# Reordering the loads, the set-up additions and the late transposes of an embedding-and-cross-layer kernel on one core

## The reference

```python
e = jnp.stack([tbl_0[ids[:, 0]], ..., tbl_25[ids[:, 25]]], axis=1)      # 512 x 26 x 32
x1 = jnp.einsum('bik,bjk,hij->bhk', e, e, W1) + b1[None, :, None]       # 128 features
x2 = jnp.einsum('bik,bjk,hij->bhk', x1, e, W2) + b2[None, :, None]      # 128 features
z = jnp.sum(jnp.concatenate([x1, x2], axis=1), axis=-1)                 # 512 x 256
h = jnp.concatenate([z, dense_ctx], axis=1)                             # 512 x 272
h = jnp.maximum(h @ W_top1 + b_top1, 0.0)                               # 512 x 512
h = jnp.maximum(h @ W_top2 + b_top2, 0.0)                               # 512 x 256
y = h @ W_top3                                                          # 512 x 1
```

## Time and profile before

| | |
|---|---|
| median of 3 runs | 177.65 us (177.57 to 177.9) |
| profiled execution | 177.05 us, of which the span is 175.3 us |
| PE busy | 155.5 us (89% of the span) |
| DVE busy | 117.2 us (67%) |
| ACT busy | 74.5 us (43%) |
| POOL busy | 72.8 us (42%) |
| mean granted TensorE clock | 0.961 of full speed |
| bytes moved | 8.71 MB, nearly all in the first 22 us |

### The profile page before, as it was taken

One profiled execution on the slowest core, in us unless ns is written; L12 is line 12 of the kernel. 1 busy time (PEld: TensorE's weight loads), 2 busy tenths in 40 slices (PEclk: granted clock), 3 DMA queues, 4 the chain that ended last, 5 costly groups with the idle time before them and its releaser, 6 DMA issues.

```text
span 175.3 us, 3331 instructions
## 1 busy us (share of the span) xinstructions
PE 155.5 (89%) x1273; PEld 147.0 (84%) x1273; DVE 117.2 (67%) x371; ACT 74.5 (43%) x188; POOL 72.8 (42%) x80
## 2 busy tenths in 40 slices
PE   6549999920999968999899999989999998999995
PEld 6449999910999967999799999979999997999993
DVE  5073748999979994699866669985666996432000
ACT  0205454800595543065555406455540645753022
POOL 2605065545665584545565455466555300000000
PEclk9978999995599999999999999999999999999999
DMA  3999910000000000001000000000000000000000
GB/s 98 410 399 397 351 46 12 9 8 11 11 11 10 9 11 8 11 9 15 11 8 15 8 9 14 13 11 8 15 8 9 14 0 0 6 0 0 4 0 0
DMA packets 4626, 8.71 MB, mean 50 GB/s; under 512 B 1761, under 2 KB 3425, under 8 KB 4354
## 3 DMA queue, kind: packets, MB, share of 16 engines
q1 hardware_dynamic: 1410, 3.63, 5.6%
q10 hardware_dynamic: 896, 3.68, 5.5%
q0 software_dynamic: 2304, 1.18, 4.8%
HBM read 8.49 MB, written 0.00 MB: 48 GB/s over the span
## 4 chain that ended last, share of the span: by engine, by line
PE 70%; DVE 15%; ACT 6%; DMA 5%; issue 2%; SPq 0%
PE bank L337 14%; DVE folded L680 8%; PE bank L345 8%; PE bank L283 8%; PE bank L350 7%; PE bank L354 7%; PE bank L299 6%; DMA w2t<-in_w2t_dram 5%; PE bank L358 5%; PE bank L377 2%; PE bank L375 2%; ACT diag L504 2%; PE bank L364 2%; PE bank L310 2%; ACT h L512 2%
## 5 line engine op out<-in xcount | busy, mean ns | idle before, releaser
L257 POOL DMA_INDIRECT rows<-in_tbl_dram,idx x72 | 72.0, 1000 | 64.1 <-DMA rows<-in_tbl_dram,idx 45.8
L337 PEld LDWEIGHTS bank<-diag,prod 128*128 128x128 f32 x256 | 30.5, 192 | 2.0 <-issue 1.5
L337 PE MATMUL bank<-diag,prod 128*128 128x108 f32 x256 | 31.4, 276 | 0.5 <-issue 0.2
L669 DVE COPY t<-bank 13x128 f32<-13x128 f32 (+1 forms) x64 | 16.8, 263 | 19.3 <-PE bank L345 18.6
L504 ACT ACTIVATE diag<-prod,quad 128x416 f32<-128x416 f32 (+1 forms) x32 | 17.5, 620 | 17.4 <-DVE prod L632 17.4
L485 ACT COPY t<-bank 128x432 f32<-128x432 f32 x32 | 15.0, 522 | 23.1 <-PE bank L337 23.1
L283 PE MATMUL bank<-small,onehot 128*128 128x256 f32 (+1 forms) x64 | 19.8, 412 | 1.4 <-DVE w1p L617 1.4
L617 DVE TENSOR_TENSOR w1p<-bank,chosen 128x320 f32<-128x320 f32 (+2 forms) x24 | 13.1, 547 | 10.9 <-PE bank L283 10.6
L345 PE MATMUL bank<-diag,prod 128*77 128x64 f32 x256 | 20.1, 230 | 0.0
L345 PEld LDWEIGHTS bank<-diag,prod 128*77 128x77 f32 x256 | 19.4, 149 | 0.0
L492 ACT COPY t<-bank 55x256 f32<-55x256 f32 (+2 forms) x48 | 14.1, 294 | 2.7 <-PE bank L345 2.3
(11 more groups left out here) (71 smaller groups left out, 197.3 us busy)
## 6 DMA issues: line engine op xcount, KB each, us to landing
idb<-in_idt_dram ACTq DMA_DIRECT2D x1, 1536.0 KB, 17.4
rows<-in_tbl_dram,idx POOLq DMA_INDIRECT x72, 2.4
small<-in_small_dram SPq DMA_DIRECT2D x1, 1120.0 KB, 12.1
wt<-in_W_top_dram SPq DMA_DIRECT2D x2, 512.0 KB, 17.5
w2t<-in_w2t_dram ACTq DMA_DIRECT2D x1, 832.0 KB, 8.1
w2t<-in_w2t_dram SPq DMA_DIRECT2D x1, 832.0 KB, 9.5
w1t<-in_w1t_dram ACTq DMA_DIRECT2D x1, 640.0 KB, 13.5
w1p<-in_w1p_dram SPq DMA_DIRECT2D x1, 521.0 KB, 7.4
```

The source lines that it names most:

```text
L257: pool.indirect_dma_start(rows[t][:, f, :], None, tables[f], bass.IndirectOffsetOnAxis(ap=idx[:, t, f:f + 1], axis=0)).then_inc(s_got[t][p ...
L337: mm = nc.tensor.matmul(m0[:, g % GBANK, :, 0:JW], prod[:, G, 0:P], diag[:, G, :, :], start=True, stop=True)
L669: ins = nc.vector.tensor_copy(t1[p0:p0 + HALF, GRAM + slot:GRAM + slot + nb, n], m1[64:64 + HALF, :].rearrange("p (n j) -> p j n", n=NSTEP ...
```

## The change

Loads: the indices come in one transfer; `idb` for tile 0 moves from the head of ACT's queue to behind `w1p` on SP's; `w2t` comes in three pieces, all at the head of ACT's queue. DVE: two memsets of `t1` go to the front, the first `one_hot` behind `w1s` and `chosen`; the additions to `b2x32` and `z1w` go behind tile 0's picks; low and cross_a additions go ahead of `half_a(0)`; the cross_b additions go between `half_b(0)`, `bands(0, 0)` and `bands(0, 1)`; all picks of tile 1 go behind the four `bands` of tile 0. PE: the look-ups of tile 0 stand behind later set-up jobs; the v0 jobs of fields 0 to 12 go behind steps 1 and 2 of tile 0, in banks 6 and 7; the look-ups of tile 1 go behind tile 0's four steps, the last one behind `z1`; `layer3(t - 1)` goes behind `step(t, 0)`, with its `copy_y`. ACT: two spreads ahead of `relu2` and two behind it. POOL: of 18 gathers a tile the waits come after 5, 9, 13 and 18.

```diff
-BURST = 3
+PAUSES = [(0, 8), (0, 12), (1, 20), (2, 25)]
+W2PARTS = [(0, 6), (6, 14), (14, 26)]
-HOME = [RING[q % len(RING)] for q in range(DONE["ctB"])] + [0, 1, 2, 0] + [3, 4, 5, 7] + [0, 1, 2, 0]
+HOME = [RING[q % len(RING)] for q in range(DONE["ctB"])] + [0, 1, 2, 0] + [3, 4, 5, 7] + [6, 7, 6, 7]
-BEHIND = {6: 0, 8: 1, FOLDS - 1: 2, FOLDS: 3, FOLDS + 1: 4, FOLDS + 2: 5}
+BEHIND = {10: 0, 12: 1, FOLDS: 2, FOLDS + 1: 3, FOLDS + 2: 4, FOLDS + 3: 5}
@@ sync
-            sp.dma_start(idx[:, 0, :], io["ids"][:, 0, :]).then_inc(s_idx[0], 16)
+            sp.dma_start(idx[:], io["ids"]).then_inc(s_idx, 16)
             sp.dma_start(w1p[:], io["w1p"]).then_inc(s_w1p, 16)
-            sp.dma_start(w2t[:, 0:HALF, :], io["w2t"][:, 0:HALF, :]).then_inc(s_w2[0], 16)
+            sp.dma_start(idb[:, 0, :], on_all(io["idt"], 0, 1)).then_inc(s_idb[0], 16)
@@ gpsimd
-                        if f > g0 and (f - g0) % BURST == 0:
-                            pool.wait_ge(s_got[t][part], 16 * (f - g0))
+                        if (part, f) in PAUSES:
+                            if part == 2:
+                                pool.wait_ge(s_got[t][1], 16 * (PARTS[1][1] - PARTS[1][3]))
+                            pool.wait_ge(s_got[t][part], 16 * (f + 1 - g0))
-                    pool.wait_ge(s_got[t][part], 16 * (f1 - g0))
@@ tensor, look_up, make and step
+                if t == 1 and pick < 2:
+                    pe.wait_ge(s_sf, len(SETUP))
+                    if x0 == 0:
+                        pe.wait_ge(s_pb, PRODS)
+                    if t and s == 0 and g == GBANK:
+                        pe.wait_ge(s_h2, t * MT2)
@@ tensor, the tiles
                     step(t, s)
-                    if more:
-                        if s == 0 and t == 0:
-                            pe.wait_ge(s_sf, DONE["v1"])
+                    if t and s == 0:
+                        layer3(t - 1)
+                    if t and more:
                         look_up(t + 1, s)
+                    if t == 0 and s in (1, 2):
+                        for q in range(DONE["v1"] + 2 * s - 2, DONE["v1"] + 2 * s):
+                            make(q)
+                pe.wait_ge(s_e0, (t + 1) * STEPS)
                 if t == 0:
-                    pe.wait_ge(s_e0, STEPS - 1)
-                    pe.wait_ge(s_e1, STEPS - 1)
-                    pe.wait_ge(s_eg, STEPS - 1)
-                    for q in range(DONE["v1"], len(SETUP)):
-                        make(q)
-                    pe.wait_ge(s_sf, len(SETUP))
+                    look_up(1, 0)
+                    look_up(1, 1)
                 z2_low(0, 6)
+                if t == 0:
+                    look_up(1, 2)
                 z2_low(6, HALF)
+                if t == 0:
+                    look_up(1, 3)
                 z2_high(t)
+                    look_up(1, 4)
                 z1()
+                if t == 0:
+                    look_up(1, 5)
                 layer1(t)
                 layer2(t)
-                layer3(t)
+            layer3(TILES - 1)
@@ scalar
-            act.dma_start(idb[:, 0, :], on_all(io["idt"], 0, 1)).then_inc(s_idb[0], 16)
-            act.dma_start(w2t[:, HALF:FIELDS, :], io["w2t"][:, HALF:FIELDS, :]).then_inc(s_w2[1], 16)
-            act.dma_start(idx[:, 1:TILES, :], io["ids"][:, 1:TILES, :]).then_inc(s_idx[1], 16)
+            for i, (j0, j1) in enumerate(W2PARTS):
+                act.dma_start(w2t[:, j0:j1, :], io["w2t"][:, j0:j1, :]).then_inc(s_w2[i], 16)
+                    if s == 0 and t:
+                        copy_y(t - 1)
+                    if t == 0 and s in (1, 2):
+                        for q in range(DONE["v1"] + 2 * s - 2, DONE["v1"] + 2 * s):
+                            take(q)
-                    spread(t + 1, 1, range(0, 3))
+                    spread(t + 1, 1, range(0, 2))
                 relu2(t)
-                    spread(t + 1, 1, range(3, QUADS))
+                    spread(t + 1, 1, range(2, QUADS))
@@ vector, tile 0
+            nc.vector.tensor_scalar(b2x32[:], vec[:, 0:1], float(EMB), None, ALU.mult).then_inc(s_pad, 1)
+            nc.vector.tensor_tensor(z1w[:], w1t[:, 0, :, :], w1t[:, 1, :, :], ALU.add).then_inc(s_z1w, 1)
-            half_a(0)
...
+            half_a(0)
             half_b(0)
             cross = cross_b(folded, ct[1])
-            for t in range(TILES):
+            add(cross, 0, False)
+            bands(0, 0)
+            add(cross, 1, True)
+            bands(0, 1)
+            one_hot(1)
+            bands(0, 2)
+            bands(0, 3)
+            for i in range(len(PICKS)):
+                pick(1, i)
+            half_a(1)
+            half_b(1)
+            for t in range(1, TILES):
```

More of the change, by code:

```diff
@@ L180, in arrive @@
         def arrive(t, pick):
-            return bank[6 + pick % 2] if t == 0 else bank[7]
-        s_idx = [sem(f"s_idx{i}") for i in range(2)]
+            return bank[6 + pick % 2] if t < 2 else bank[7]
+        s_idx = sem("s_idx")
         s_got = [[sem(f"s_got{t}_{part}") for part in range(3)] for t in range(TILES)]
@@ L187, in dlrm_tower @@
         s_idb = [sem(f"s_idb{i}") for i in range(2)]
-        s_w2 = [sem(f"s_w2{i}") for i in range(2)]
+        s_w2 = [sem(f"s_w2{i}") for i in range(len(W2PARTS))]
         s_iota = sem("s_iota")
@@ L273, in look_up @@
                     pe.wait_ge(s_oh, t + 1)
[L274 to L278, removed]
+                if t == 0 and pick == 0:
+                    pe.wait_ge(s_small, 16)
+                if t == 1 and pick < 2:
+                    pe.wait_ge(s_sf, len(SETUP))
+                if t < 2:
+                    if t or pick >= 2:
+                        pe.wait_ge(s_pick, t * len(PICKS) + pick - 1)
                 else:
@@ L311, in make @@
                 elif kind == "v1":
-                    if HOME[q] == 7:
+                    if HOME[q] >= 6:
                         pe.wait_ge(s_pick, len(PICKS))
@@ L534, in _ @@
                 if t == 0:
-                    for q in range(DONE["v1"], len(SETUP)):
-                        take(q)
                     act.wait_ge(s_vec, 32)
@@ L545, in _ @@
                 if t < TILES - 1:
-                    spread(t + 1, 1, range(0, 3))
+                    spread(t + 1, 1, range(0, 2))
                 relu2(t)
                 if t < TILES - 1:
-                    spread(t + 1, 1, range(3, QUADS))
-                copy_y(t)
+                    spread(t + 1, 1, range(2, QUADS))
+            copy_y(TILES - 1)
         @block.vector
@@ L580, in one_hot @@
                                         ALU.is_equal).then_inc(s_oh, 1)
+            link(nc.vector.memset(t1[:, GRAM:GRAM + GSLOTS, :], 0.0))
+            link(nc.vector.memset(t1[32:64, 0:GRAM, :], 0.0))
             dve.wait_ge(s_iota, 2)
@@ L585, in _ @@
             linked()
[L586 to L590, removed]
+            dve.wait_ge(s_idx, 16)
             link(nc.vector.tensor_scalar(part_of[:], idx[:], CBITS, None, ALU.logical_shift_right))
@@ L593, in _ @@
             link(nc.vector.tensor_copy(partf[:], part_of[:]))
+            dve.wait_ge(s_w1p, 16)
+            nc.vector.tensor_tensor(w1s[:], w1p[:, 0, :], w1p[:, 1, :], ALU.add).then_inc(s_w1s, 1)
             linked()
@@ L599, in _ @@
             ins.then_inc(s_ch, 1)
-            link(nc.vector.memset(t1[:, GRAM:GRAM + GSLOTS, :], 0.0))
-            link(nc.vector.memset(t1[32:64, 0:GRAM, :], 0.0))
-            dve.wait_ge(s_vec, 32)
-            nc.vector.tensor_scalar(b2x32[:], vec[:, 0:1], float(EMB), None, ALU.mult).then_inc(s_pad, 1)
-            dve.wait_ge(s_w1t, 16)
-            nc.vector.tensor_tensor(z1w[:], w1t[:, 0, :, :], w1t[:, 1, :, :], ALU.add).then_inc(s_z1w, 1)
+            one_hot(0)
             def pick(t, i):
@@ L708, in _ @@
                         pick(t + 1, s)
-                    if t == 0 and s < 2:
-                        add(cross, s, s == 1)
                 if more:
```

15 lines of the change are left out of this document (7 added, 8 removed).

## The result

The changed kernel took 191.37 us, the median of 4 runs (187.96 to 194.47), beside 177.78 (177.57 to 178.49) for the kernel before: a ratio of 1.062 [1.051, 1.073]. It is slower, as forecast, but by 13.6 us where the sum said 7.1, and outside the range of 180.8 to 188.2. The ratio is taken from the two shorter of its runs (187.96 and 189.94); the profiled execution, 192.80, is one of the two longer ones, which the median takes in. Its own runs lie 6.5 us apart, those of the kernel before 0.9. That is the first hint: nothing in the forecast was of a kind that changes from run to run.

A forecast was written before the change was run, and what follows sets the result against it. PE's busy stream was taken as the bound, with DVE's list setting the path until tile 1's products. Terms of 6.0 plus 1.1 for the clock gave +7.1 on the profiled 177.05, 184.2, so 184.7 us; range 180.8 to 188.2.

The forecast's parts named there:

- Gathers ... Priced 0: POOL's gathers: four waits a tile instead of six save some 1.4 us each, rows land in time for DVE; priced 0.
- The start: Folds at the kernel's start: PE starts at about 9.5, 1.8 us earlier; tile 0's step 0 at 47.2.
- The wait for cross_b: Behind tile 0's step 1: PE idles 4 us until 57.3; `z2_low` starts at 66.7 instead of 68.41.
- the rule on transposes: A skill's rule: transposes don't bring the full clock, ending tile 0's early steps up to 2.5 us later; not used.
- Tile 1's first step: Step (1, 0) waits for DVE's late product pieces and starts at 88.0 against 84.87: +3.1 us.
- +0.8 for the clock at this boundary: Tile 1's boundary: PE idles twice and may return at the lower clock; 0 to +2.5, taken as +0.8 us.
- `one_hot(2)`, +1.5: DVE late again in tile 1: `look_up(2, 0)` comes 4.6 behind the step's start against 3.1, +1.5 us.
- Layer 3, 0.5 + 0.9: Layer 3 behind the next tile's first step, in PE's busy stream: +0.5 us in tile 2, +0.9 in tile 3.
- C: Rival: tile 1's products are in time; 179.0 us, or 177.1 with the start at full clock; chance 0.1.
- A: Rival: the clock holds, full from 9.5 us on and after each wait; 181.8 us; chance 0.2.
- B: Rival: PE's clock falls every time it idles; 188.7 us; chance 0.12.
- D: Rival: the reorder gives nothing at the start, `w1p` held by the longer index transfer; 187.5 us; chance 0.08.

The follow-up runs named there:

- e14: Kernel before with only the gathers' waits changed, to bursts of five, four, four and five, on the fourth chip: 185.45 us, ratio 1.034.
- e5: Changed kernel, unchanged, run again on the second chip: 184.07 us, ratio 1.035, no late updates.
- e18: Changed kernel, unchanged, run once more on the fifth chip: 183.71 us, ratio 1.033.
- e3: Kernel before with only layer 3 and its copy moved behind the next tile's first step, and two and two spreads around the second relu: 180.89 us, 1.019.
- e8: Changed kernel with tile 1's look-ups and picks back in tile 0's steps and layer 3 back in its own tile: 177.13 us, 0.998.
- e13: Changed kernel with POOL waiting after every three gathers again, on the fourth chip: 186.51 us, ratio 1.038.
- e16: Kernel before with the loads reordered and the long gather bursts in tile 0 alone, on the fifth chip: 173.70 us, 0.977.

## Why the prediction was wrong

**The step that failed is "Gathers ... Priced 0".** It asked only whether the rows land in time for DVE, and they do. It did not ask what more gathers in flight do to others. On the chips where the effect shows, they make TensorE's semaphore updates late: 5.9 us by e14 alone, on one of them. In the first trace the late updates and the low clock behind one of them account for the 8.7 us by which it is longer than e5's. That the long bursts made those updates late too is inferred: on the chip of the first runs no bursts of three were tried in the changed kernel. Without late updates the forecast's total holds, by errors that cancel: 184.07 and 183.71 on two chips (e5, e18), where the sum said 184.7. The range had no rival of this kind.

**The start: right in kind, too small.** The folds start at 7.57, not 9.5. `w1p` landed sooner: the `w1s` addition starts at 6.81 instead of 8.73, 1.9 us earlier, where the bound said "up to 1 us more". The clock was full from there to the end of the folds (the first trace's 44 fold instructions ran in 7.09, 0.16 each, against 0.22 before), where the forecast took half of that gain. The first step came at 43.78 instead of 47.2. DVE's list had the length forecast: from the last look-up's end to the step, 20.6 us (23.21 to 43.78) against 20.5.

**The wait for cross_b: right.** From `half_b(0)`'s end to the transposes, e5 has 46.95 to 53.92, so 7.0, where the forecast had 50.4 to 57.3, so 6.9. Then it reckoned 9.4 to `z2_low` and +1.2 for the clock; e5 has 10.9 (53.92 to 64.85), so the clock cost 1.5. The forecast did well not to use the rule on transposes: in e5 the granted clock was 0.50 from 35 to 38 and 1.00 from 39 on, while PE had run nothing but transposes since 34.94.

**Tile 1's first step: right time, wrong reason.** Forecast 88.0, measured 88.80 in e5. But it was reckoned from a `half_a(1)` at 79.2, which came at 76.96, and with DVE's pieces last, which were ready at 85.8. What ended last was ACT: the Z2 copy behind `spread(1, 0)`, then layers 1 and 2 at the low clock. The forecast saw that queue ("the copy of Z2, and so layer 1, is queued behind it"), and called it a tie because it placed PE's layers at the full clock; its +0.8 for the clock at this boundary stood apart, as if it came on top of DVE's pieces. Two errors of opposite sign, the early start and ACT's queue, met.

**`one_hot(2)`, +1.5: not there.** Because the step waited for ACT, DVE was all but through its pieces when it began (they end at 88.95). Tile 1 lasted 31.86 in e5, no more than tile 2 (31.85), so nothing of its own was left of this term.

**Layer 3, 0.5 + 0.9: too small.** Every later tile lasts 1.0 longer than the 30.84 before, and e3 costs 3.1 us by itself. About half of it is PE's busy time (0.53 for layer 3's four instructions), as forecast. Most of the rest is the spread order, which the forecast called "only in another order". The timeline of e3:

```profile
82.45 1.03 ACT L510 ACTIVATE diag<-prod,quad 128x320 f32<-128x320 f32 x2
83.72 0.63 ACT L523 ACTIVATE h<-bank,vec 128x128 f32<-128x128 f32 x2 [0.24 <-PE bank L389]
84.23 1.04 ACT L510 ACTIVATE diag<-prod,quad 128x320 f32<-128x320 f32 x2
85.37 2.01 PE L339 MATMUL bank<-diag,prod 128*128 128x108 f32 x16 [1.47 <-issue]
```

After two spreads `relu2` is too early and waits 0.24 for layer 2. Two spreads stand behind it instead of one, so the last ends at 85.27, against 84.77. The step is 0.5 later than 84.87 (0.15 of it has come from tile 0, `z2_low` starting at 68.56 instead of 68.41), and layer 3 then stands between PE's busy steps. With three spreads ahead ACT had filled that wait.

**The rivals.** None named what happened. C needed tile 1's products not to be last at the boundary, and e8's 84.31 shows that it takes another order to get there. A needed the full clock after each wait. In e5 the step behind the cross_b wait took 3.02, which refutes it. In the first trace that step took 1.77, but there the clock was low from 36 to 49, and again from 108 to 114. B's 188.7 is the nearest to the first runs, but for another reason, and D's late start did not come.

**Open.** What makes the updates late is not settled. The runs show that gathers in bursts of 4 and 5 bring it about or make it much longer (e13 keeps a little of it with bursts of 3), and that it takes certain chips, or certain times: it is there in two of the five sets and in the first runs, and each set is one chip at one time. The kernel before is 1 to 2 us slower in those two sets as well (179.1 and 179.6 against 177.4 to 177.9), but not in the first runs (177.8). They don't show whether the path is shared with the gathers' descriptors or with the landing rows, nor whether the recording of the times takes part. e16 was not tried on a chip that shows late updates; only in tile 0 would long bursts be exposed there.

## What to carry to other kernels

- A longer burst of indirect gathers isn't free because the rows land in time. Look for waits by an idle engine on work that is long done, and time it on more than one chip before it is kept.
- When work is brought forward, find the queue that sets the second event as well. Here the same DVE list set step 0 and cross_b, and the 6 us won at step 0 were given back before tile 1; with DVE's order left alone, the reordered loads and tile 0's longer bursts kept 4.2 us by the medians (e16).
- Price a tie at the clock that the idle before it leaves: a copy queued behind a late spread cost 2.8 us beyond DVE's list.

## What the runs showed of the hardware

TensorE's semaphore updates can come some 3 us after its matmuls end (3.5 for ACT and 2.5 for DVE in the first trace, 3.3 for ACT in e14), to two engines at nearly the same moment, in kernels that keep four or five indirect gathers in flight. The profile then names a "remote" releaser on a one-core kernel, or puts the wait down to the matmuls that have long ended. The same kernel, the changed one, took from 183.7 to 191.8 us by median over four sets and the first runs, where the kernel before stayed within 177.4 to 179.6. The long bursts alone in the kernel before give a ratio of 0.999 on a chip without late updates (e2) and 1.034 on one with them (e14).
